# Row tiles of 32 for the transposed score matmuls, issued two at a time

## What is computed

```
q = (LN(x) @ w_q.T).reshape(B, S, 8, 4, 8)        # 8 groups of 4 heads, 8 wide
k, v = (ctx @ w_k.T), (ctx @ w_v.T)               # one per group
scores = einsum('bnghd,bmgd->bnghm', q, k) / sqrt(8)
attn = softmax(causal(pad(scores)), axis=-1)
out = einsum('bnghm,bmgd->bnghd', attn, v) @ w_o.T + b_o
```

## Time and profile before

| | |
|---|---|
| median of 3 runs | 410.42 us (410.26 to 411.62) |
| profiled execution, span | 407.7 us |
| PE busy | 342.2 us, 84% |
| DVE busy | 214.7 us, 53% |
| ACT busy | 159.8 us, 39% |
| POOL busy | 98.1 us, 24% |
| chain of waits by engine | PE 57%, DVE 20%, ACT 8%, issue 7% |
| attention's weights and values, batches 0 to 3 | about 187 to 309 us |
| TensorE clock over the span | 0.937 of full |

### The profile page before, as it was taken

The page is one execution under the profiler, slowest core; times in us unless marked ns, Lnnn a source line. Parts: engine busy times, 40 slices in busy tenths (PEclk is TensorE's granted clock), DMA queues, the critical chain, the costliest instruction groups (busy, mean ns, idle before and its releaser), DMA issues.

```text
span 407.7 us, 4559 instructions
## 1 busy us (share of the span) xinstructions
PE 342.2 (84%) x1471; PEld 205.9 (50%) x1477; DVE 214.7 (53%) x509; ACT 159.8 (39%) x336; POOL 98.1 (24%) x148
## 2 busy tenths in 40 slices
PE   2799775509999848989799989979889879999997
PEld 1385565405656526545454555444443434444886
DVE  1544885601222248879446934881241338679921
ACT  1443221204333123145873875477873223333000
POOL 4402553330000256301340442054450001000000
PEclk9999998558999666999999999998999999999999
DMA  7995000134111115400000000000000000000011
GB/s 234 365 426 105 1 13 2 40 124 146 41 51 53 39 47 175 191 6 0 9 0 2 0 6 2 0 2 8 0 2 0 2 0 0 0 0 2 13 51 39
DMA packets 13879, 22.40 MB, mean 55 GB/s; under 512 B 2033, under 2 KB 11249, under 8 KB 13042
## 3 DMA queue, kind: packets, MB, share of 16 engines
q1 hardware_dynamic: 13090, 20.03, 14.5%
q0 software_dynamic: 768, 2.10, 1.6%
HBM read 15.83 MB, written 6.03 MB: 54 GB/s over the span
## 4 chain that ended last, share of the span: by engine, by line
PE 57%; DVE 20%; ACT 8%; issue 7%; DMA 3%; POOL 3%; another core or an unknown queue 1%; SPq 0%; DVEq 0%; ACTq 0%; POOLq 0%
PE bank L229 43%; DVE mx L1151 9%; PE bank L439 5%; ACT region L875 5%; PE bank L407 3%; DVE stats L946 2%; POOL x_sorted L692 2%; PE bank L242 1%; DMA ctxT<-in_ctxT_dram 1%; DVE x_sb L986 1%; PE bank L410 1%; PE bank L236 1%; PE bank L453 1%; PE bank L487 1%; ACT xT L747 1%
## 5 line engine op out<-in xcount | busy, mean ns | idle before, releaser
L1151 DVE TENSOR_REDUCE mx<-bank 128x2 f32<-128x512 f32 (+1 forms) x96 | 59.8, 684 | 14.0 <-PE bank L410 7.8
L875 ACT ACTIVATE region<-bank,padcol 128x512 f32<-128x512 f32 x96 | 60.8, 701 | 12.6 <-PE bank L229 11.6
L730 POOL TENSOR_SCALAR_AFFINE_SELECT region<-region 128x1024 f32<-128x1024 f32 x32 | 35.0, 1094 | 94.6 <-ACT region L875 94.3
L229 PE MATMUL bank<-xT,e_gu 128*128 128x512 f32 x128 | 56.6, 594 | 0.5 <-ACT xT L747 0.5
L229 PE MATMUL bank<-qst,kblk 128*128 128x512 f32 x96 | 46.1, 507 | 1.6 <-ACT region L875 0.7
L407 PE MATMUL bank<-kblk,qst 128*128 128x512 f32 x96 | 43.4, 475 | 1.7 <-DVE mx L1151 0.9
L229 PEld LDWEIGHTS bank<-xT,e_gu 128*128 128x128 f32 x128 | 23.8, 190 | 28.0 <-issue 27.1
L664 POOL TENSOR_SCALAR veps<-mv 128x1 f32<-128x1 f32 x40 | 11.3, 284 | 80.8 <-DVE mv L948 80.5
L410 PE MATMUL bank<-causb,identb 128*128 128x256 bf16 (+1 forms) x90 | 28.3, 314 | 0.0
L229 PE MATMUL bank<-e_down,region 128*128 128x256 f32 x128 | 27.8, 379 | 0.0
L986 DVE SCALAR_TENSOR_TENSOR x_sb<-bank,tg,x_sb 128x256 f32<-128x256 f32 x24 | 11.6, 482 | 29.2 <-PE bank L229 28.9
(11 more groups left out here) (155 smaller groups left out, 546.6 us busy)
## 6 DMA issues: line engine op xcount, KB each, us to landing
e_gu<-in_e_gu_dram SPq DMA_DIRECT2D x2, 1408.0 KB, 12.4
x_sorted<-zero SPq DMA_DIRECT2D x1, 1920.0 KB, 9.9
y_sorted<-region SPq DMA_DIRECT2D x15, 128.0 KB, 1.7
x_sb<-in_x_dram SPq DMA_DIRECT2D x4, 256.0 KB, 6.1
ctxT<-in_ctxT_dram SPq DMA_DIRECT2D x2, 512.0 KB, 6.1
e_down<-in_e_down_dram SPq DMA_DIRECT2D x1, 1024.0 KB, 14.3
region<-x_sorted SPq DMA_DIRECT2D x1, 1024.0 KB, 7.3
e_gu<-in_f_gate_dram SPq DMA_DIRECT2D x1, 1024.0 KB, 4.8
```

The lines of the kernel that those rows point to most:

```text
L229: return pe.matmul(dst, lhsT, rhs, start=first, stop=last)
L730: pool.affine_select(out=block, in_=block, compare_op=ALU.is_ge, fill=0.0, base=0, pattern=[[0, 2], [0, PER_GROUP], [1, P]], channel_multi ...
L875: taken(act.activation(dst, src.rearrange("p (h n) -> p h n", n=SEQ - mt * P), ACT.Exp, bias=padcol[:, key:key + 1], scale=float(HD) ** -0 ...
L1151: taken(dve.reduce_max(mx[:, b % 2, nt, quads, q, hg], src, AX), "sa")
```

## The change

Three edits. `weights` takes the 32 rows of its quad from both operands instead of all 128, so the matmul occupies one group of 32 rows of the array. `weight_fill` lets the quad run fastest, so that fills n and n+1 (n even) are on neighbouring quads. PE's loop issues `scores` n+12 and n+13, then `weights` n and n+1, and then, each at its own n, what else belongs to the two steps. ACT writes the exponentials in the new order, and POOL's first clearing of a half waits for 8 exponentials instead of 4.

```
         def weight_fill(n):
             q, c = divmod(n, 12)
-            return (q, c // 2, 0, slice(c % 2 * 2, c % 2 * 2 + 2)) if c < 8 else (q, c - 8, 1, slice(0, 4))
+            return (q, c % 4, 0, slice(c // 4 * 2, c // 4 * 2 + 2)) if c < 8 else (q, c - 8, 1, slice(0, 4))
...
-                ready(mm(dst, kblk[s][q][:, j, tile_cols(mt)], qst[:, s, q, heads, mt * P:SEQ], True, True), "sb")
+                group = slice(32 * j, 32 * j + 32)
+                ready(mm(dst, kblk[s][q][group, j, tile_cols(mt)], qst[group, s, q, heads, mt * P:SEQ], True, True), "sb")
...
-                    if b + 1 < BATCH and n + LEAD < 24:
-                        scores(b + 1, n + LEAD)
-                    weights(b, n)
+                    if n % 2 == 0:
+                        for m in (n, n + 1):
+                            if b + 1 < BATCH and m + LEAD < 24:
+                                scores(b + 1, m + LEAD)
+                        weights(b, n)
+                        weights(b, n + 1)
                     if b >= 1 and n % 2 == 1:
                         finish(b - 1, n // 2)
...
-                        pool.wait_ge(sem("sb_taken"), 24 * b + 12 * q + (4, 8, 10, 12)[n])
+                        pool.wait_ge(sem("sb_taken"), 24 * b + 12 * q + (8, 8, 10, 12)[n])
```

## The result

The changed kernel takes **426.07 us** (median of 4 runs, 423.54 to 432.0) against 410.8 us (410.26 to 411.62) for the kernel before on the same chip. The ratio is 1.0351, 95% interval 1.0328 to 1.0375: slower by 3.5%, where +1.3 us (0.3%) was forecast and the range ended at 416.0.

A forecast was written before the change was run, and what follows sets the result against it. DVE was taken to bound the first halves, ACT the second halves and batch 3. The terms 0.6 + 0 + 0.4 + 0.1 + 0.2 = +1.3 us on 410.42 gave 411.7 us, range 409.3 to 416.0.

The forecast's parts named there:

- the first halves: First halves of batches 0, 1 and 2: PE's longer pairs against DVE's pace cost +0.6, 0 and +0.4 us.
- the third rival: Weights on 32 rows don't hold PE's clock; it falls after batches 0, 1, 3: 416.8 us, chance 0.15.
- Two weights at once: A pair's two weights on neighbouring row groups run together on PE, in 0.25 us (bounds 0.24 to 0.48).
- The second rival: Two row groups don't run at once, so each pair costs 0.24 us more: 415.3 us, chance 0.13.
- The change of form: PE switching between full rows and a row group costs 0.20 us each way, 0.40 us a pair.
- The first rival: Changing form is free for row groups of 32, so the kernel is not slower: 409.9 us, chance 0.22.
- POOL and the order: Clearings of a half end about one clearing (1.09 us) later, +0.2 us; the order's gains lie in batch 1.
- the moved turn and weight: Batch 1, first half: last score not behind the queries' turn (-0.3 us), n = 15 weight (0.24) before the projection.
- Second halves and batch 3: ACT sets the pace there, so changes of form hide in slack: +0.1 us (-0.3 to +0.5).
- the main sum: All terms of the forecast over the whole kernel together: +1.3 us.

The follow-up runs named there:

- e2_tiles_no_pairs: The kernel before with one edit: each weight on the 32 rows of its quad, order as before; 442.82 us, ratio 1.0776.
- e3_tiles_first_halves: The changed kernel with 32-row tiles only in the first halves of batches 0 to 2, other weights on 128 rows; 413.73 us, ratio 1.0081.
- e1_pairs_full_rows: The changed kernel with the weights on all 128 rows again, pairing and order kept; 411.78 us, ratio 1.0014.
- e4_tiles_weight_only: The changed kernel with 32-row tiles only in second halves and batch 3, other weights on 128 rows; 425.77 us, ratio 1.0368.
- e5_twice_32_rows: The changed kernel with 32-row tiles only in second halves and batch 3, each such weight issued twice; 435.12 us, ratio 1.0569.

## Why the prediction was wrong

The forecast summed PE's work against DVE's in the first halves and took the clock as it was. That sum came out near, about 2 us where 1.0 was forecast for the first halves; the clock, kept as the third rival with a chance of 0.15, decided.

**The steps that held.** PE's timeline of the changed kernel, one pair after another in batch 0 with narrow masks, and then from batch 1 with the two turns of `finish`:

```profile
192.01 0.50 PE L229 MATMUL bank<-qst,kblk 32*128 32x512 f32 x2
192.44 0.50 PE L407 MATMUL bank<-kblk,qst 128*128 128x512 f32 x1
...
193.36 0.50 PE L229 MATMUL bank<-qst,kblk 32*128 32x512 f32 x2
...
231.73 0.50 PE L229 MATMUL bank<-qst,kblk 32*128 32x512 f32 x2
232.16 0.44 PE L454 MATMUL bank<-ident,prod 128*128 128x128 f32 x2
...
233.24 0.50 PE L229 MATMUL bank<-qst,kblk 32*128 32x512 f32 x2
```

- *Two weights at once.* The entry of two lasts 0.50 us, as long as a single one in `e2_tiles_no_pairs`; they start 3 to 4 ns apart, in all 18 pairs of the first halves. The second rival is out. It was argued from column tiles, and row tiles do the same, as the Trainium skill says (TensorE: Matmul & The Clock Gate, Part 3); here that holds for two tiles, four were not tried. In the weight-only stretches 14 of 30 pairs start together too, more than the forecast's "rarely at work at once".
- *The change of form.* From the two weights to the next score 192.44 - 192.01 = 0.43 us pass, one stream and a change. The pair is 193.36 - 192.01 = 1.35 us, forecast 1.35; with turns 233.24 - 231.73 = 1.51, forecast 1.56. The first rival, no cost for 32 rows, is out too, and by the unpaired kernel's 0.39 for two changes the price is 0.20 each.
- *The first halves.* DVE's run of maxima in batch 0 now has breaks that the mask causes:

```profile
191.75 3.38 DVE L1155 TENSOR_REDUCE mx<-bank 128x2 f32<-128x512 f32 x5 [0.17 <-PE bank L410]
```

On the page, idle time before the maxima that is put down to the mask went from 7.8 to 15.1 us; full rows in the new order show 14.1, so that number alone tells little. The stage lengths of `e3_tiles_first_halves` against those of `e1_pairs_full_rows` tell more: 36.4 to 34.8 in batch 0, 39.4 to 38.8 in batch 1, 25.7 to 25.5 in batch 2. That is +1.6, +0.6 and +0.2 us where +0.6, 0 and +0.4 were forecast; the first two lie beyond their bounds of 1.0 and +0.4. In batch 0 a piece of 3.4 us at half clock is part of it:

```profile
204.00:207.40 3.40, 3.40 (x7) 2.09 (x8) 0.00 (x0) 3.24 (x6) 2.40 (x3) 0.50 0.05 15
```

- *POOL and the order.* Forecast +0.2 for POOL and -0.5 for the moved turn and weight; full rows in the new order give 1.0014, that is +0.6 us with an interval that holds zero. Not more than their bounds allowed, and not told apart.

**The step that failed: "Second halves and batch 3 ... +0.1 (-0.3 to +0.5)".** Its reasoning was of slack: ACT frees a bank every 0.59 us, a change of form has room to hide in. That is true as long as the clock stands: ahead of the falls the tiles cost at most 0.4 us a batch. But the kernel with tiles in just these stretches is 14 us slower than with full rows. The term was not 0.1 but about +14, nearly all of it by way of the clock.

**The rival that came true was sized too low.** It said that weights on 32 of 128 rows don't hold the clock, that it falls behind batches 0, 1 and 3 and over `values`, for 3.4 us each time, 1.7 us each. The mechanism is confirmed by `e4_tiles_weight_only`, by `e5_twice_32_rows` and by the kernel with full rows beside the tiles. Two numbers in it were wrong:

- *How long it lasts.* 3.4 us was the one fall in the kernel before. The pieces are 10, 7, 10 and 17 us. The fall outlasts the tiles: the last weights of batch 0 end at 207.1, and the keys and queries behind them, on all 128 rows but for two matmuls of `padrow`, still run at 0.50 until 215.4 with PE busy throughout. At the end of batch 2, which the rival left out, the 3.4 us of the kernel before became 10, and in batch 3 it came inside and not only after it.
- *What it costs.* 1.7 us for 3.4 is the bound for a PE that is the only limit. Between the changed kernel and `e3_tiles_first_halves` the four stages differ by 3.0, 2.0, 2.8 and 4.2 us, 12.0 in all, for 44.3 - 6.8 = 37.5 us more at half clock: 0.32 us per us, not 0.5. That error alone would have made the price too high; the duration, off by a factor of two to five, outweighed it.

The argument against the rival, "PE is in use as long as before", failed twice. At the end of batch 0 PE was in use less (1.72 of 3.2 us, against 2.77 of 3.4 before). And in batch 3, where it was in use for 5.72 of 5.8 us, the clock fell all the same, as it did with each weight twice. The evidence for it, "the weights are all that PE does there", deserved more than 0.15: the trace of the kernel before had no stretch with only part of the rows at work, so it could speak neither way, and PE is the bound of the keys, queries and values that follow. A rival that can't be judged from the rows and costs several times the main sum should have widened the range to its own worst case: the clock at half over all of keys, queries and values.

**What stays open.** Which mixture of rows and time in use holds the clock. 64 rows once behaved as 32, 64 rows twice as 128 in batch 3 only, and elsewhere PE was mostly in use for too little of the time to tell. Why the clock came back after 3.4 us in one kernel and after 10 to 17 in another, with PE busy in both, was not tested either. One full-row matmul a pair was enough in three places and in one execution, and not in the fourth place.

## What to carry to other kernels

Before putting matmuls on part of the array's rows, look for stretches in which nothing else runs on PE, and for what follows them: there the saved PE time can be lost several times over through the clock, also in later full-row work. Full-row matmuls in between are no safeguard by themselves: with pairs of tiles between scores the clock stayed at 1.00 through the changed kernel's first halves, with single tiles between scores it was lost for 17.1 us. Read the granted clock of the stretch before keeping tiles in it. Put tiles of one form together, since each change of form cost 0.20 us, and don't add them at all where another engine is the bound. Where PE waits anyway, discarded full-row matmuls can raise the clock of what comes next; here that gave 0.5%.

## What the runs showed of the hardware

- Two fp32r matmuls of 512 columns on neighbouring groups of 32 rows start 3 to 4 ns apart, where both have their bank, and take the time of one (0.50 us by the trace). In the first halves the row tiles save one stream of 0.24 us in every pair and give back 0.40 us in two changes of form.
- A change between full rows and a row group costs 0.20 us (1.09 against 0.70 us a step with two of them). The Trainium skill (TensorEngine Tiling (Array Packing), Key Properties) has the rule that changing the mode drains the engine; the trace agrees in that every change costs time, and the figure is the trace's.
- The granted clock depended on how many rows the matmuls used: with PE busy in all of 21.2 us, on weights of 32 rows and the turns of `finish`, it had a mean of 0.58, with PE busy in 14.56 of 17.5 us on 128 rows it was 1.00. Over 72 matmuls in batch 3, with each weight issued twice, it was 1.00 on 64 rows (PE busy 17.06 of 17.3 us) and 0.58 on 32.
- It depended on the time in use too: behind weights on 128 rows it fell to 0.50 for 3.4 us where PE had been busy 1.70 of 3.4 us (`e3_tiles_first_halves`) and 1.62 of 3.4 (the kernel before), and stayed at 1.00 where PE had been busy 2.77 of 3.4.
- Single weights of 32 rows between full-row scores did not hold it: 0.50 for 17.1 us with PE busy 16.92 (`e2_tiles_no_pairs`).
- Once down behind batch 0, the clock stayed at 0.50 for 10.1 us with PE never idle, the last 8.3 us of it in keys and queries on full rows (two one-row matmuls among them). Where PE is the bound this costs about half its length (0.86 us for 1.6 to 1.8 us of `values`), over the stages as a whole 0.32 us per us.
- The same kernel can differ from execution to execution by several us along with its mean clock: the one with full rows beside the tiles took 419.78 and 420.04 us at 0.926 and 424.71 us at 0.911.
